# TensorE runs on the identity until the operands come, four key tiles are begun with their first halves, and three steps of the first batch trade places

## Chip, cores and metric

One core of one Trainium2 chip. The metric is the time of one execution on the device, in microseconds. TensorE (PE in the profile) multiplies, ScalarE (ACT) and VectorE (DVE) do the element work, GpSimd (POOL) fills and scatters, SyncE (SP) issues most of the loads.

## What is computed

A gated cross-attention layer and a layer of experts, all in fp32:

```python
def layer(x, ctx):                     # x: 16 x 100 x 512, ctx: 16 x 722 x 512
    q = (layernorm(x) @ Wq.T + bq)     # 16 heads of 32
    k, v = ctx @ Wk.T + bk, ctx @ Wv.T + bv
    o = softmax(q @ k.T / sqrt(32) + mask) @ v
    x = x + tanh(g_xattn) * (o @ Wo.T + bo)
    h = layernorm(x)
    gates = softmax(h @ gate_w + gate_b)         # 8 experts, the best 2 of each row
    y = w3[e] @ gelu(w2[e] @ gelu(w1[e] @ h + b1[e]) + b2[e]) + b3[e]
    return x + tanh(g_ffn) * sum(gates[e] * y for e in best_two)
```

## The kernel before

A stage for attention runs over 16 batches of 100 queries and 722 context rows, and a stage for the experts follows. Each engine has its own program, written out in order by hand; semaphores join them. Nothing is planned at run time in the stretch at hand.

**Products.** An fp32 product is made of three faster ones: each operand is split into a high part (a ScalarE copy, `w_high`, `ctx_high`, `k_high`) and a low part (a VectorE subtraction of the high part, `wk_low`, `ctx_low`, `k_low`), and `PRODUCTS` names the three pairs. So a key tile, 128 rows of K.T by one half of the context (362 or 360 columns), is 4 pieces `c` of the 512 inputs by 3 products: 12 matmuls into one bank of PSUM. `FRONT` are the first two pieces and `BACK` the last two. A value tile is 12 matmuls of 512 columns. Transposes and the query products are plain fp32; in the trace a plain fp32 matmul has two records and two weight loads.

**Units and banks.** Of the 8 banks, four (0 to 3) take the scores of the four heads of a group, two (4, 5) the transposed probabilities, and two (6, 7) everything else: the units. A unit is one such result: `K20` is key tile 2 of context half 0, `V1` value tile 1, `XT` the transposed normed rows, `Q` the queries, `A2` the attention output of group 2. `PROLOGUE`, `FIRST_BODY`, `EVEN_BODY` and `ODD_BODY` list them in order, and the loop below them gives each its bank, alternately, and its number of fill. TensorE waits in `bank_for` until the unit before in that bank has been emptied; for a key tile that is after ScalarE's `keys_high` and VectorE's `keys_low`. In the prologue `XT` and `Q` have a third bank, score bank 0, which is free until the first scores.

**Prologue.** It makes the keys, three value tiles and the queries of batch 0. SyncE asks for the first half of the key weights, the first two pieces of the context, the second half of the weights, the other two pieces, then the value weights, the second half of the context, the rows `x_ln` to be normed, and so on. ScalarE and VectorE split them in that order: `w_lo` counts the low halves of the weights (1 and 2 for the keys, 3 and 4 for the values), `ctx_lo` those of the context. TensorE waits for `w_lo` 1 and `ctx_lo` 1, runs `FRONT` of key tiles 0 and 1, waits for `w_lo` 2 and `ctx_lo` 2, runs their `BACK`, then tiles 2 and 3 whole. GpSimd makes the 128x128 identity `ident` in its first instructions (`ident_step` 2).

**A batch.** Four groups of four heads. For each: `scores` for each context half into four banks, VectorE's `score` takes them out, adds the mask and finds the maximum; ScalarE's `exps`, one for each head; TensorE's `transpose_probs`, which needs the `copy_probs` of the head before, as there is one pair of banks for it; and `attend`. Between them TensorE has the next batch's key and value tiles as filling. `scores` of a half wait until VectorE has taken out the half before. In batch 0 the order around the change is:

- ScalarE, heads 8 to 11: `keys_high` of tile 2, `copy_probs` 10 and 11, `rstd_start(0, 2)` (logarithm and exponential of the variance of batch 2's rows), `keys_high` of tile 0, half 1.
- VectorE: `wo_lower` (low part of the output weights, a whole 128x2048), `keys_low` of tile 2, `norm_in(2)` (statistics of batch 2's rows), `recips(2)`, `keys_low` of tile 0 half 1, `ln_apply(0, 2)` (three steps on one column, and the normed rows `xn`), then the scores of group 3.
- ScalarE, heads 12 to 15: `copy_probs` 13, `keys_high` of tile 1 half 1, `exps` 15, `copy_probs` 14 and 15.

SyncE loads batch 2's rows `x_ln` once batch 1's are normed. GpSimd, once for each of the first score groups, starts a transfer of 3341 KB that fills a region of the expert rows.

Of the kernel before, what the change touches and what calls it, by code (L numbers as in the profile page):

```python
# [16 lines left out]
P = 128  # L17
# [195 lines left out]
             "A0", "A1", "X2T", "A2", "LG", "CNT")  # L213
LAST_TURNS = LAST_BODY.index("A0")
PRO = -1
SAME_BANK = {("LG", "A1"), ("CNT", "A2"), ("XT", "A2")}


ALL_UNITS = {}
FILLS = [0, 0, 0]  # L220
_next = 0
for body in range(PRO, B + 1):
    _names = {PRO: PROLOGUE, 0: FIRST_BODY, B - 2: LAST_QUERIES, B - 1: LAST_BODY, B: AFTER_LAST
              }.get(body, ODD_BODY if body % 2 else EVEN_BODY)
    for _i, name in enumerate(_names):
        if _i > 0 and (_names[_i - 1], name) in SAME_BANK:
            _next = 1 - _next
        if body >= B - 1:
            _bank = _i % 2 if body == B else (_i + 1) % 2 if _i < LAST_TURNS else 0
        elif body == PRO and name in ("XT", "Q"):  # L230
            _bank = 2
        else:
            _bank, _next = _next, 1 - _next
        FILLS[_bank] += 1
        ALL_UNITS[body, name] = _bank, FILLS[_bank]
# [36 lines left out]
def attention(nc, sem, shared_from, bank_rows, banks, ident, block_expert, block_row, early,  # L272
              xs_dram, x, ctx_in, mask, g_x, g_f, wq, bq, wk, bk, wv, bv, wo, bo, gw, gb, out,
              w1, b1, w2, b2, w3, b3):
    score_bank, pt_bank, unit_bank = banks[0:4], banks[4:6], banks[6:8] + banks[0:1]

    bk_loaded = sem("bk_loaded")
    bv_loaded = sem("bv_loaded")
# [21 lines left out]
    xres_loaded = sem("xres_loaded")  # L300
    ctx_hi = sem("ctx_hi")
    ctx_lo = sem("ctx_lo")
    filled = [sem("unit_bank_0_filled"), sem("unit_bank_1_filled"), sem("first_queries_filled")]
    emptied = [sem("unit_bank_0_emptied"), sem("unit_bank_1_emptied"), sem("first_queries_emptied")]
    k_hi = sem("k_hi")
    ln_step = [sem("ln1_step"), sem("ln2_step")]
    ln_log = [sem("ln1_log"), sem("ln2_log")]
# [347 lines left out]
    def on_tensor(pe):  # L655
# [314 lines left out]
        def last_body(b, odd):  # L970
# [76 lines left out]
            for m in range(4, HT):  # L1047
                early_second(m)

        pe.wait_ge(ident_step, 2)  # L1050
        pe.wait_ge(pt_zero, 1)
        pe.wait_ge(w_lo, 1)
        pe.wait_ge(ctx_lo, 1)
        keys(PRO, 0, 0, 0, FRONT)
        keys(PRO, 0, 1, 0, FRONT)
        pe.wait_ge(w_lo, 2)
        pe.wait_ge(ctx_lo, 2)
        keys(PRO, 0, 0, 0, BACK)
        keys(PRO, 0, 1, 0, BACK)
        keys(PRO, 0, 2, 0)  # L1060
        keys(PRO, 0, 3, 0)
        pe.wait_ge(w_lo, 4)
        values(PRO, 0)
        values(PRO, 1)
# [14 lines left out]
    def on_scalar(act):  # L1079
# [29 lines left out]
        def keys_high(body, n, m, half):  # L1109

            if n > 0:
                act.wait_ge(scores_ready, 2 * DT * (n - 1) + 2 * m + half + 1)
            bank, _ = take(body, f"K{m}{half}")
            off, size = HALVES[half]
            nc.scalar.activation(k_hl[0][:, m, off:off + size], bank[:, 0:size], ACT.Identity,  # L1115
                                 bias=bk_sb[:, m:m + 1]).then_inc(k_hi, 1)
# [45 lines left out]
        def first_body():  # L1162

            b, n = 0, 1
            half_used(PRO, "V2")
            ctx_high(n, 0)
            ctx_high(n, 1)
            keys_high(b, b, 3, 1)
            exps(b, 0)
            exps(b, 1)  # L1170
            copy_probs(b, 0)
            exps(b, 2)
            copy_probs(b, 1)
            exps(b, 3)
            copy_probs(b, 2)
            copy_probs(b, 3)
            rstd_start(0, 1)

            half_used(b, "V5")
            ctx_high(n, 2)  # L1180
            ctx_high(n, 3)
            recip_copy(b, 0)
            exps(b, 4)
            exps(b, 5)
            copy_probs(b, 4)
            exps(b, 6)
            copy_probs(b, 5)
            exps(b, 7)
            keys_high(b, n, 0, 0)
            copy_probs(b, 6)  # L1190
            copy_transposed(b, "XS", xt[:, :, slot(1), :])
            copy_probs(b, 7)
            wo_upper()

            keys_high(b, n, 1, 0)
            recip_copy(b, 1)
            exps(b, 8)
            exps(b, 9)
            copy_probs(b, 8)
            exps(b, 10)  # L1200
            copy_probs(b, 9)
            exps(b, 11)
            keys_high(b, n, 2, 0)
            copy_probs(b, 10)
            copy_probs(b, 11)
            rstd_start(0, 2)
            keys_high(b, n, 0, 1)

            keys_high(b, n, 3, 0)
            copy_transposed(b, "XT", xt[:, :, slot(2), :])  # L1210
            recip_copy(b, 2)
            exps(b, 12)
            exps(b, 13)
            queries_high(b, "Q01")
            copy_probs(b, 12)
            exps(b, 14)
            copy_probs(b, 13)
            keys_high(b, n, 1, 1)
            exps(b, 15)
            copy_probs(b, 14)  # L1220
            copy_probs(b, 15)
            keys_high(b, n, 2, 1)

# [182 lines left out]
    def on_vector(dve):  # L1406
# [288 lines left out]
        def first_body():  # L1695
# [27 lines left out]
            score(b, 2, 1)  # L1723
            scale_o(b, b, 1)
            values_out(b, 1, 2)
            wo_lower()
            keys_low(b, n, 2, 0)
            norm_in(2)
            recips(b, 2)
            keys_low(b, n, 0, 1)  # L1730
            ln_apply(0, 2, x_ln[:], xn[:], xn_ready)

            score(b, 3, 0)
            keys_low(b, n, 3, 0)
            score(b, 3, 1)
            scale_o(b, b, 2)
            queries_low(b, "Q01")
            keys_low(b, n, 1, 1)
            recips(b, 3)
            keys_low(b, n, 2, 1)  # L1740
# [983 lines left out]
```

## Time and profile before

| | us |
|---|---|
| median of 3 runs (lowest, highest) | 1788.13 (1786.92, 1789.49) |
| profiled execution | 1788.08 |
| its span | 1786.1 |
| TensorE busy in the span | 1760.7 |
| VectorE busy | 1168.8 |
| ScalarE busy | 961.6 |

Times in the profile are counted from the start of the span. The profiled execution took 2.0 us more than its span. Busy time of TensorE includes matmuls that overlap, so it doesn't tell how near the engine is to its peak; the spacing of the starts does.

### The profile page before, as it was taken

Reading aid. Unit: us, or ns where it says so; the run is one execution under the profiler, and the core shown is the slowest. Engines: PE = TensorE matmul, PEld = TensorE weight load, DVE = VectorE, ACT = ScalarE, POOL = GpSimd, SP = SyncE. Lnnn points to the kernel's source line nnn. Section 1 sums busy time; section 2 is a strip of 40 time slices with the busy share of each in tenths; the row PEclk is TensorE's granted clock in tenths of the full one; section 3 lists DMA queues with packets and bytes.
Section 4 is the critical chain, followed back from the end, with each engine's and each line's share of the span. In section 5 each row is a group of like instructions: output and inputs, shape, how many; then the busy total and the mean of one; then the engine's idle time right before and its main releaser. Section 6 shows DMA issues by size and latency. Waiting matters only on the chain.

```text
span 1786.1 us, 39483 instructions
## 1 busy us (share of the span) xinstructions
PE 1760.7 (99%) x14832; PEld 1530.9 (86%) x14832; DVE 1168.8 (65%) x3158; ACT 961.6 (54%) x1794; POOL 119.6 (7%) x159
## 2 busy tenths in 40 slices
PE   8999999999999999999999999999999999999997
PEld 7788888888888888888888877877899999999996
DVE  5666666666667666666666456556677777777772
ACT  4565655555565656555555535445555555455551
POOL 1000000000000000000000010100001111111110
PEclk9999999999999999999999999999999999999999
DMA  7991111111111211111103489999666666767761
GB/s 244 338 336 43 48 49 42 48 48 52 38 48 49 59 38 48 48 49 47 40 16 95 152 278 396 372 346 310 212 209 206 212 209 217 217 217 217 213 199 36
DMA packets 114267, 269.72 MB, mean 151 GB/s; under 512 B 15283, under 2 KB 33715, under 8 KB 114128
## 3 DMA queue, kind: packets, MB, share of 16 engines
q1 hardware_dynamic: 99664, 225.46, 38.0%
q0 software_dynamic: 14464, 42.35, 8.2%
q8 instruction: 94, 1.54, 0.4%
q14 instruction: 45, 0.37, 0.1%
HBM read 221.10 MB, written 46.66 MB: 150 GB/s over the span
## 4 chain that ended last, share of the span: by engine, by line
PE 95%; DMA 2%; DVE 1%; ACT 1%; issue 1%; POOL 0%; DVEq 0%; SPq 0%; ACTq 0%; POOLq 0%
PE bank_rows L2304 21%; PE bank_rows L688 15%; PE bank_rows L674 15%; PE bank_rows L736 8%; PE bank_rows L2319 6%; PE bank_rows L726 5%; PE bank_rows L747 4%; PE bank_rows L2358 4%; PE bank_rows L2385 3%; PE bank_rows L2344 3%; PE bank_rows L711 3%; PE bank_rows L763 3%; PE bank_rows L826 2%; DMA stage<-in_L_ffn_w 1%; PE bank_rows L750 1%; PE bank_rows L812 1%
## 5 line engine op out<-in xcount | busy, mean ns | idle before, releaser
L1139 ACT ACTIVATE probs<-probs,neg_max 100x722 f32<-100x722 f32 x248 | 220.9, 891 | 101.0 <-DVE neg_max L1491 101.0
L1484 DVE CUSTOM_DVE_ANT_0 probs<-bank_rows,mask_sb 100x362 f32<-100x362 f32 x496 | 234.6, 529 | 11.5 <-PE bank_rows L726 7.2
L2548 DVE TENSOR_TENSOR w_low<-stage,w_high 128x1024 fp32r<-128x1024 f32 x176 | 212.9, 1223 | 33.9 <-ACT w_high L2452 32.9
L1144 ACT ACTIVATE p_t<-bank_rows 121x600 f32<-121x600 f32 x256 | 171.9, 672 | 77.4 <-PE bank_rows L736 73.9
L2475 ACT ACTIVATE gelu<-bank_rows,biases 128x256 f32<-128x256 f32 x176 | 82.4, 475 | 222.9 <-PE bank_rows L2304 189.5
L2452 ACT ACTIVATE w_high<-stage 128x1024 fp32r<-128x1024 f32 x176 | 183.7, 1057 | 31.4 <-DMA stage<-in_L_ffn_w 31.4
L2304 PE MATMUL bank_rows<-h_low,w_high 128*128 128x256 f32 x704 | 199.2, 283 | 0.0
L2304 PE MATMUL bank_rows<-h_high,w_low 128*128 128x256 f32 x704 | 199.2, 283 | 0.0
L2304 PE MATMUL bank_rows<-h_high,w_high 128*128 128x256 f32 x704 | 199.2, 283 | 0.0
L674 PE MATMUL bank_rows<-ctx_high,wk_high 128*128 128x360 f32 (+1 forms) x512 | 183.8, 359 | 8.6 <-DVE ctx_low L1450 8.1
L736 PE MATMUL bank_rows<-ident,probs 100*121 100x100 f32 x1488 | 180.6, 257 | 1.6 <-ACT p_t L1144 1.4
L736 PEld LDWEIGHTS bank_rows<-ident,probs 100*121 100x121 f32 x1488 | 160.4, 156 | 23.6 <-issue 2.2
L674 PE MATMUL bank_rows<-ctx_low,wk_high 128*128 128x360 f32 (+1 forms) x512 | 168.9, 330 | 0.0
L674 PE MATMUL bank_rows<-ctx_high,wk_low 128*128 128x360 f32 (+1 forms) x512 | 168.4, 329 | 0.0
L1457 DVE SCALAR_TENSOR_TENSOR k_low<-bank_rows,bk_sb,k_high 128x362 fp32r<-128x362 f32 (+1 forms) x128 | 76.1, 594 | 131.3 <-ACT k_high L1115 117.1
L688 PE MATMUL bank_rows<-wv_high,ctx_high 128*120 128x512 f32 (+1 forms) x384 | 161.7, 421 | 0.0
L688 PE MATMUL bank_rows<-wv_high,ctx_low 128*120 128x512 f32 (+1 forms) x384 | 151.1, 394 | 0.0
L688 PE MATMUL bank_rows<-wv_low,ctx_high 128*120 128x512 f32 (+1 forms) x384 | 151.0, 393 | 0.0
L2304 PEld LDWEIGHTS bank_rows<-h_high,w_low 128*128 128x128 f32 x704 | 135.2, 192 | 0.0
L2304 PEld LDWEIGHTS bank_rows<-h_high,w_high 128*128 128x128 f32 x704 | 135.1, 192 | 0.0
L2304 PEld LDWEIGHTS bank_rows<-h_low,w_high 128*128 128x128 f32 x704 | 135.1, 192 | 0.0
L1115 ACT ACTIVATE k_high<-bank_rows,bk_sb 128x362 fp32r<-128x362 f32 (+1 forms) x128 | 72.0, 563 | 112.7 <-PE bank_rows L674 112.7
(244 smaller groups left out, 3718.8 us busy)
## 6 DMA issues: line engine op xcount, KB each, us to landing
stage<-in_L_ffn_w SPq DMA_DIRECT2D x240, 512.0 KB, 4.5
plain_w<-in_L_ffn_w SPq DMA_DIRECT2D x15, 2048.0 KB, 12.3
expert_in_rows<-filling POOLq DMA_DIRECT2D x8, 3341.0 KB, 15.2
ctx_raw<-in_ctx SPq DMA_DIRECT2D x16, 720.0 KB, 4.9
ctx_raw<-in_ctx SPq DMA_DIRECT2D x15, 724.0 KB, 4.3
xs_sb<-expert_in_rows SPq DMA_DIRECT2D x11, 514.0 KB, 5.1
b_sb<-in_L_ffn_b SPq DMA_DIRECT2D x19, 256.0 KB
mask_sb<-in_mask_BxSxS_ff SPq DMA_DIRECT2D x16, 282.0 KB
```

Source lines behind the costliest of these rows:

```text
L674: last = nc.tensor.matmul(bank[:, 0:size], wk_hl[a][:, c, m * P:(m + 1) * P], ctx_t[b][half][:, c, :], start=(c == 0 and s == 0), stop=(c ...
L688: last = nc.tensor.matmul(bank[0:rows, :], ctx_t[a][half][:, c, off:off + rows], wv_hl[b][:, c, :], start=(c == 0 and s == 0), stop=(c == ...
L726: last = nc.tensor.matmul(score_bank[q][0:S, 0:size], q_t[a][rows, g, slot(b), :], k_hl[c][rows, g, off:off + size], start=(step == 0), st ...
L736: last = nc.tensor.transpose(pt_bank[i // 3][0:rows, i % 3 * S:(i % 3 + 1) * S], probs_of(b, h // HQ)[:, h % HQ, off:off + rows], ident[0: ...
L1139: nc.scalar.activation(p, p, ACT.Exp, bias=neg_max[:, h:h + 1], scale=-1.0, accum_out=exp_sum[:, h:h + 1]).then_inc(probs_ready, 1)
L1144: nc.scalar.activation(p_t[:, h % HQ, :, :].rearrange("t (k i) s -> t k (i s)", k=2), bank_rows[0:TT, 4:6, 0:3 * S], ACT.Copy).then_inc(pt ...
L1484: nc.vector.tensor_tensor_reduce(out=probs_of(b, g)[:, q, at], in0=score_bank[q][0:S, 0:size], in1=mask_sb[:, at], scale=-1.0, scalar=BIG, ...
L2304: last = nc.tensor.matmul(mm_bank[m % 4][:, 0:BLOCK], w[a][:, k, m * P:(m + 1) * P], src[c][:, k, :], start=(k == 0 and s == 0), stop=(k = ...
L2319: last = nc.tensor.matmul(y_bank[t][:], h_hl[1][a][:, k, t * P:(t + 1) * P], w_hl[2][c][:, k, :], start=(k == 0 and s == 0), stop=(k == HT ...
L2452: nc.scalar.activation(hi, src, ACT.Copy).then_inc(chunk_hi[which], 1)
L2475: nc.scalar.activation(gelu[:, m % 2, :], mm_bank[m % 4][:, 0:BLOCK], ACT.Gelu, bias=bias_of(n, layer, m)).then_inc(g_done, 1)
L2548: nc.vector.tensor_tensor(lo, src, hi.bitcast(F32), ALU.subtract).then_inc(chunk_lo[which], 1)
```

## The change

- A run-up: once the identity is made, TensorE multiplies it by itself 15 times into score bank 3. Nothing reads the result.
- `K20` and `K30` of the prologue get banks of their own, score banks 0 and 1, so that four key tiles are open at once. All four are begun with `FRONT`, then all four are finished with `BACK`. `XT` and `Q` follow in score bank 0.
- Batch 0, VectorE: `norm_in(2)` goes ahead of tile 2's `keys_low`, `ln_apply(0, 2)` ahead of `recips(2)` and of tile 0's `keys_low`, and `wo_lower` behind `queries_low`.
- Batch 0, ScalarE: `rstd_start(0, 2)` goes ahead of `copy_probs` 10, and tile 1's `keys_high` behind `copy_probs` 14.

```diff
--- before.py
+++ after.py
@@ -213,11 +213,12 @@
              "A0", "A1", "X2T", "A2", "LG", "CNT")
 LAST_TURNS = LAST_BODY.index("A0")
 PRO = -1
+RUN_UP = 15
 SAME_BANK = {("LG", "A1"), ("CNT", "A2"), ("XT", "A2")}
 
 
 ALL_UNITS = {}
-FILLS = [0, 0, 0]
+FILLS = [0, 0, 0, 0]
 _next = 0
 for body in range(PRO, B + 1):
     _names = {PRO: PROLOGUE, 0: FIRST_BODY, B - 2: LAST_QUERIES, B - 1: LAST_BODY, B: AFTER_LAST
@@ -227,8 +228,8 @@
             _next = 1 - _next
         if body >= B - 1:
             _bank = _i % 2 if body == B else (_i + 1) % 2 if _i < LAST_TURNS else 0
-        elif body == PRO and name in ("XT", "Q"):
-            _bank = 2
+        elif body == PRO and name in ("K20", "K30", "XT", "Q"):
+            _bank = 3 if name == "K30" else 2
         else:
             _bank, _next = _next, 1 - _next
         FILLS[_bank] += 1
@@ -272,7 +273,7 @@
 def attention(nc, sem, shared_from, bank_rows, banks, ident, block_expert, block_row, early,
               xs_dram, x, ctx_in, mask, g_x, g_f, wq, bq, wk, bk, wv, bv, wo, bo, gw, gb, out,
               w1, b1, w2, b2, w3, b3):
-    score_bank, pt_bank, unit_bank = banks[0:4], banks[4:6], banks[6:8] + banks[0:1]
+    score_bank, pt_bank, unit_bank = banks[0:4], banks[4:6], banks[6:8] + banks[0:2]
 
     bk_loaded = sem("bk_loaded")
     bv_loaded = sem("bv_loaded")
@@ -300,8 +301,9 @@
     xres_loaded = sem("xres_loaded")
     ctx_hi = sem("ctx_hi")
     ctx_lo = sem("ctx_lo")
-    filled = [sem("unit_bank_0_filled"), sem("unit_bank_1_filled"), sem("first_queries_filled")]
-    emptied = [sem("unit_bank_0_emptied"), sem("unit_bank_1_emptied"), sem("first_queries_emptied")]
+    filled = [sem("unit_bank_0_filled"), sem("unit_bank_1_filled"), sem("unit_bank_2_filled"), sem("unit_bank_3_filled")]
+    emptied = [sem("unit_bank_0_emptied"), sem("unit_bank_1_emptied"),
+               sem("unit_bank_2_emptied"), sem("unit_bank_3_emptied")]
     k_hi = sem("k_hi")
     ln_step = [sem("ln1_step"), sem("ln2_step")]
     ln_log = [sem("ln1_log"), sem("ln2_log")]
@@ -1047,18 +1049,19 @@
             for m in range(4, HT):
                 early_second(m)
 
+
         pe.wait_ge(ident_step, 2)
+        for _ in range(RUN_UP):
+            nc.tensor.matmul(score_bank[3][:, 0:P], ident[:], ident[:], start=True, stop=True)
         pe.wait_ge(pt_zero, 1)
         pe.wait_ge(w_lo, 1)
         pe.wait_ge(ctx_lo, 1)
-        keys(PRO, 0, 0, 0, FRONT)
-        keys(PRO, 0, 1, 0, FRONT)
+        for m in range(DT):
+            keys(PRO, 0, m, 0, FRONT)
         pe.wait_ge(w_lo, 2)
         pe.wait_ge(ctx_lo, 2)
-        keys(PRO, 0, 0, 0, BACK)
-        keys(PRO, 0, 1, 0, BACK)
-        keys(PRO, 0, 2, 0)
-        keys(PRO, 0, 3, 0)
+        for m in range(DT):
+            keys(PRO, 0, m, 0, BACK)
         pe.wait_ge(w_lo, 4)
         values(PRO, 0)
         values(PRO, 1)
@@ -1201,9 +1204,9 @@
             copy_probs(b, 9)
             exps(b, 11)
             keys_high(b, n, 2, 0)
+            rstd_start(0, 2)
             copy_probs(b, 10)
             copy_probs(b, 11)
-            rstd_start(0, 2)
             keys_high(b, n, 0, 1)
 
             keys_high(b, n, 3, 0)
@@ -1215,9 +1218,9 @@
             copy_probs(b, 12)
             exps(b, 14)
             copy_probs(b, 13)
-            keys_high(b, n, 1, 1)
             exps(b, 15)
             copy_probs(b, 14)
+            keys_high(b, n, 1, 1)
             copy_probs(b, 15)
             keys_high(b, n, 2, 1)
 
@@ -1723,18 +1726,18 @@
             score(b, 2, 1)
             scale_o(b, b, 1)
             values_out(b, 1, 2)
-            wo_lower()
+            norm_in(2)
             keys_low(b, n, 2, 0)
-            norm_in(2)
+            ln_apply(0, 2, x_ln[:], xn[:], xn_ready)
             recips(b, 2)
             keys_low(b, n, 0, 1)
-            ln_apply(0, 2, x_ln[:], xn[:], xn_ready)
 
             score(b, 3, 0)
             keys_low(b, n, 3, 0)
             score(b, 3, 1)
             scale_o(b, b, 2)
             queries_low(b, "Q01")
+            wo_lower()
             keys_low(b, n, 1, 1)
             recips(b, 3)
             keys_low(b, n, 2, 1)
```

## Rows read from the trace of the kernel before

**Rows 1.** The page: the chain of waits by engine, and the instruction queue.

```profile
q8 instruction: 94, 1.54, 0.4%
...
PE 95%; DMA 2%; DVE 1%; ACT 1%; issue 1%; POOL 0%; DVEq 0%; SPq 0%; ACTq 0%; POOLq 0%
```

**Rows 2.** What TensorE waited for in all: us in total, times, longest us.

```profile
PE bank_rows L726 <- DVE half_max L1484: 1.4, 2, 1.2
...
PE bank_rows L747 <- issue: 1.1, 1, 1.1
```

**Rows 3.** Timeline of TensorE, 7.9 to 15.5 us: start, us, what, idle before.

```profile
8.13 0.64 PE L674 MATMUL bank_rows<-ctx_high,wk_high 128*128 128x362 f32 x1 [8.13 <-DVE ctx_low L1450]
...
12.79 0.43 PE L674 MATMUL bank_rows<-ctx_high,wk_high 128*128 128x362 f32 x1
...
14.92 0.43 PE L674 MATMUL bank_rows<-ctx_high,wk_high 128*128 128x362 f32 x1 [0.36 <-DVE k_low L1457]
```

**Rows 4.** Windows in the prologue: us, busy (count) of PE, PEld, DVE, ACT, POOL, clock, DMA.

```profile
8.20:12.70 4.50, 4.50 (x15) 4.50 (x16) 3.61 (x4) 3.21 (x4) 0.00 (x0) 1.00 1.04 349
14.92:19.01 4.09, 4.09 (x24) 4.09 (x25) 2.92 (x4) 2.19 (x4) 0.00 (x0) 1.00 1.06 350
```

**Rows 5.** Timeline of all engines, 0 to 30 us.

```profile
1.28 0.29 POOL L481 TENSOR_SCALAR_AFFINE_SELECT ident<-ident 128x128 f32<-128x128 f32 x1 [0.24 <-POOL ident L479]
...
7.04 0.94 DVE L1450 TENSOR_TENSOR ctx_low<-ctx_raw,ctx_high 128x724 fp32r<-128x724 f32 x1
...
9.71 0.91 DVE L1450 TENSOR_TENSOR ctx_low<-ctx_raw,ctx_high 128x724 fp32r<-128x724 f32 x1
...
11.14 2.43 DVE L1867 TENSOR_TENSOR wv_low<-wq_sb,wv_high 128x1024 fp32r<-128x1024 f32 x2 [0.52 <-ACT wv_high L1373]
```

**Rows 6.** Chain of waits, 1129 to 1137 us: start, us, what.

```profile
1133.03 3.57 PE bank_rows L2344 x32
```

**Rows 7.** DMA of 0 to 60 us in 40 slices; one load, last number us to landing.

```profile
DMA  0599999979999999889865000004999999999999
...
wq_sb<-in_L_xattn_Wq SPq DMA_DIRECT2D x1, 1024.0 KB, 8.6
```

**Rows 8.** Chain of waits, 36 to 110 us.

```profile
80.63 0.78 PE bank_rows L736 x6
...
83.18 0.06 DVE k_low L1457
...
83.69 0.22 DVE rstd L1429
...
84.78 0.53 DVE probs L1484
...
86.83 0.74 PE bank_rows L726 x11
```

**Rows 9.** Timeline of ScalarE and VectorE, 76 to 88 us.

```profile
76.37 2.28 DVE L1693 TENSOR_TENSOR wo_low<-wo_sb,wo_high 128x2048 fp32r<-128x2048 f32 x1
...
79.81 0.67 ACT L1144 ACTIVATE p_t<-bank_rows 121x600 f32<-121x600 f32 x1
...
82.00 0.29 ACT L1103 ACTIVATE rstd<-moments,eps 100x1 f32<-100x1 f32 x1
...
82.32 0.20 ACT L1106 ACTIVATE rstd<-rstd 100x1 f32<-100x1 f32 x1
```

**Rows 10.** Timeline of ScalarE and TensorE, 94 to 98 us.

```profile
96.41 0.66 ACT L1144 ACTIVATE p_t<-bank_rows 121x600 f32<-121x600 f32 x1
...
97.22 0.77 PE L736 MATMUL bank_rows<-ident,probs 100*121 100x100 f32 x6 [0.64 <-ACT p_t L1144]
```

**Rows 11.** Timeline of SyncE's issues, 56 to 62 us.

```profile
57.47 0.32 SPq L597 DMA_DIRECT2D x_ln<-in_x  x1
```

**Rows 12.** DMA of 26 to 130 us: packets and MB of the queue; median us to landing.

```profile
q8 instruction: 7, 0.11, 0.4%
...
ctx_raw<-in_ctx SPq DMA_DIRECT2D x2, 724.0 KB, 13.1
```

## Prediction

> **What bounds the kernel now.** I read the page first. Its chain of waits says that TensorE sets the end: 95% of the chain is TensorE work [rows 1]. Then the waits of TensorE: after the first matmul has begun, its engine loses time to others in only a few places [rows 2], all of them before 98 us. The queries for 100 to 962 us name none. From there to the end the kernel is a sequence that is started by TensorE's own progress (loads wait on counters of finished work), so what TensorE gains before 98 us should reach the end unchanged. The question is then only how much earlier its instruction stream runs at 98 us.
>
> The timeline of TensorE shows two losses in the prologue. The first matmul starts at 8.13 us, when the first low half of the context is ready, and the 15 next ones stand 0.300 us apart; after 12.79 us, that is 4.66 us of work, they stand closer, and from 14.92 us there are 24 in 4.09 us, 0.170 each [rows 3, 4]. 362 columns in 0.300 us is the 1.2 GHz level, the faster spacing the 2.4 GHz level. The granted clock column says 1.00 in both stretches [rows 4], so here the spacing must be read, not the column. Second, at 14.92 us the key tiles 2 and 3 wait for the banks of tiles 0 and 1 (0.36 us idle in the row) [rows 3].
>
> **The prologue.** The run-up needs only the identity, done at 1.57 us [rows 5]. No row shows an identity matmul of this form, but the first layer of the small expert blocks has the same shape, fp32 128x128 by 128x128: 32 records in 3.57 us, two records per matmul, so 0.223 us each at the fast level [rows 6] and 0.446 us at half of that. If the clock rises 4.66 us after the start as it did before, the run-up takes 4.66 us for 10.4 matmuls and 4.6 x 0.223 = 1.03 us for the rest. It begins near 1.65 us and ends near 7.3 us, under the wait for the context's low half, which ends at 7.04 + 0.94 = 7.98 us [rows 5]. It adds nothing to the path. The bound on the other side: all 15 slow is 6.7 us, to 8.34 us, 0.2 us late. It writes a score bank that nothing uses before the first scores, moves no DMA and makes no other engine wait.
>
> Does anything feed the faster keys? First halves of four tiles are 24 matmuls, 4.09 us, to 12.22 us. The second halves need the second low half of the context, ready at 9.71 + 0.91 = 10.62 us [rows 5]: 1.6 us to spare. That is what the reordering buys: with only two tiles begun, fast matmuls would be through at about 10.2 us and stand. The four tiles hold four banks, so the wait at 14.92 us has no bank to wait for. The last 24 end at 8.13 + 8.18 = 16.31 us, against 19.01 us before [rows 4]. The gain is 2.70 us.
>
> What is late next? The values need both low halves of their weights, done at 11.14 + 2.43 = 13.57 us [rows 5], and the bank of tile 0, whose sum is complete at 13.24 us and which two copies of 0.6 us empty by about 14.6 us. Both lie ahead of 16.31 us. ScalarE and VectorE then do the copies of tiles 2 and 3 behind the second half of the context, until about 18.3 us, then the statistics; nothing takes those tiles' banks before the first transposed rows at about 26 us. TensorE has no idle time between 19 and 38 us before. The one thing that could stand still is the transfers, as they don't come earlier by this change. The DMA share by slices of 1.5 us is 0 from the 23rd slice (33 us) on, so every load asked for before has landed by about 33.5 us [rows 7]. VectorE's check for the last small loads now comes near 35.3 us (before: 38 us) and is still behind that. The query weights (1 MB) are used from 28.4 instead of 31.04 us; they are asked for when the values' weights are split, near 13.6 us, and take 8.6 us to land, so they are there near 22 us [rows 7]. I count 2.70 us, all kept. Ends for this term: 0.7 (clock slow again, below) and 2.9 (48 at the spacing inside a burst, 0.166).
>
> **Batch 0, statistics moved up.** The chain of waits shows why TensorE stands 1.2 us before the scores of group 3: VectorE gets to those scores late, at 84.78 us. It does the low key half at 83.18, and only then the layer norm's four small steps from 83.69 on, about 1.1 us [rows 8]. The low split of the output weights (2.28 us from 76.37 us) and a key copy had kept it from the statistics until 80.5 us [rows 9]. In the changed order the statistics run at 76.4 us, in the place of the split, and the norm is applied at about 80.6 us, while VectorE would wait for ScalarE anyway. The split goes behind the query halves, into idle time near 93.4 to 95.7 us, and its result is needed only in the next batch.
>
> This isn't free on ScalarE. The two statistics functions (0.29 and 0.20 us, 0.51 with the step between them) run there and now stand ahead of the copy of head 10, which began at 79.81 us; head 11's transposes began at 80.63 us, 0.15 us behind that copy's end [rows 8, 9]. So they slip to 81.14 us, and the key half behind them too: its VectorE copy goes from 83.18 to 83.69, and the group's scores on VectorE start at 84.20 instead of 84.78 us. TensorE's next scores follow at 86.25 instead of 86.83 us. TensorE's own work before them ended at 86.83 - 1.2 = 85.6 us [rows 2, 8] and ends 0.51 later now, at 86.1 us, so both arrive together. A wait of 1.2 us is replaced by one of 0.5 us earlier and 0.1 us here: gain 0.58 us. Ends: 0 (a copy I overlook) and 1.1 (if the copy of head 10 isn't held up).
>
> **Batch 0, one key copy moved down.** Before, ScalarE ran a key copy (near 95.1 us) ahead of the exponentials of head 15. The copy of head 14 then ended at 97.07 us, and head 15's transposes stood 0.64 us [rows 10]. In the new order the exponentials start near 94.6 us, the copy of head 14 ends near 96.3 us, and TensorE reaches the transposes at 96.58 us without a wait: gain 0.64 us, at most that. The key copy moves to about 96.2 us; its bank is taken again by the first key tile of the next batch some 2 us later. The split in front of its VectorE half ends before it.
>
> **Sum.** 2.70 + 0.58 + 0.64 = 3.92 us from the profiled execution's 1788.08 us (span 1786.1 and 2.0 around it) is 1784.2 us. The median of the runs is 1788.13 us, 0.05 above, which changes nothing. About 0.2%, 3.6 us, is what a measurement can tell from no change; the forecast lies just beyond it.
>
> **A rule that speaks against it.** The first 4.66 us of dense work were slow in the one execution that I have [rows 3], which doesn't say how far that moves between runs. The Trainium skill (TensorE: Matmul & The Clock Gate, "What's actually happening") says that the point at which the clock rises varies, because the chip's activity check runs free of the kernel's start, and that idle time throttles again. By the rule the run-up might end late, which costs 0.2 us, or the gap after it might undo it, which is the second rival.
>
> **Rivals.** (1) As forecast, 1784.2 us, own range 1783.4 to 1785.0.
> (2) The clock is at 1.2 GHz again, or still, when the keys begin, after the 0.8 us gap behind the run-up. Then 15.5 keys take 4.66 us and 32.5 take 5.53, to 18.3 us: gain 0.7 instead of 2.70, 1786.2 us. Against it: after the 1.2 us wait of [rows 2] the scores' 11 matmuls take 0.74 us [rows 8], with no slow stretch.
> (3) Batch 0 gives nothing back: the added ScalarE work ahead of head 10 costs what the rest brings, or the norm's rows aren't there. 1785.4 us. The load was issued at 57.47 us [rows 11] and is now needed 19 us behind its issue instead of 23; the bigger context loads of that stretch took 13.1 us in the median [rows 12]. It would have to take over 19 us to be felt at all.
> (4) TensorE stood 1.1 us near 72 us with no releaser, in the middle of a run of small matmuls, the row of [rows 2] with 1.1 us. The page counts 94 instruction transfers of 1.54 MB, 16 KB each [rows 1]. If the wait is a late one of these, the run-up's 60 or so instructions (two weight loads and two matmuls for each of 15) shift every block against the program. It may vanish: 1784.2 - 1.1 = 1783.1 us.
> (5) The other side: the same mechanism at more places. Seven transfers of that queue fall between 26 and 130 us, where DMA is busiest [rows 12]. At 1.1 us for each that comes late, four more (4.4 us) eat the whole gain; six more give 1784.2 + 6.6 = 1790.8 us, slower. For it: the shift is certain. Against: before, one of the seven stood. The Trainium skill (Runtime: NRT & Kernel Launch, "Instruction fetch mechanics") says blocks of 16 KiB are fetched ahead and mostly hidden; the page's sizes agree.
>
> **Chances.** (1) 0.60, (2) 0.08, (3) 0.12, (4) 0.12, (5) 0.08, half of it to beyond the old time. Faster by over 0.2% means under 1784.6 us: four fifths of (1), all of (4), 0.60 together. Slower by over 0.2%: 0.04. The rest, 0.36, lies within. The range takes in (2) and (3) above and (4) below, each with the half microsecond that runs differ: 1782.4 to 1787.0 us; (5) stays outside.
>
> **What would show it.** Right: 30 identity records between 1.6 and 7.5 us, with a step in their spacing near 6.3 us; the first key at 8.13 us, its successors 0.166 apart; the values at 16.3 us instead of 19.01; the first scores near 34.7 instead of 37.4 us; in batch 0 the wait before the scores of group 3 nearly gone and a new one of half a microsecond before head 11's transposes; the wait before head 15's gone. Wrong: keys 0.300 apart after 8.13, a first key later than 8.4 us, TensorE rows with idle time and no releaser, or a gain at 98 us that isn't found at 962 us.

## The result, and the profile after

| | before | changed |
|---|---|---|
| median of 7 runs (lowest, highest), us | 1787.97 (1786.92, 1789.49) | 1781.53 (1781.32, 1782.14) |
| profiled execution, span | 1788.08, 1786.1 | 1782.03, 1780.0 |
| ratio to before | | 0.9965, 95% interval 0.9955 to 0.9975 |

The change makes the kernel 6.4 us faster by the medians and 6.1 us by the two profiled executions. I had forecast 3.9 us, and 1782.4 us as the low end. The direction came out, and so did the two mechanisms that I had counted; the size did not. Part of the 6.4 us is how the seven runs of the kernel before fell: in the three larger sets (17, 28 and 33 runs) that ran beside the kernels below its median is 1787.2 to 1787.5 us, which leaves 5.7 to 6.0 us.

First what TensorE waits for in the changed kernel, in the form of [rows 2]:

```profile
PE bank_rows L1055 <- POOL ident L483: 1.6, 1, 1.6
PE bank_rows L738 <- ACT p_t L1147: 1.3, 2, 0.8
PE bank_rows L676 <- DVE ctx_low L1453: 0.7, 1, 0.7
...
PE bank_rows L728 <- DVE half_max L1487: 0.2, 1, 0.2
```

The wait of 1.2 us for the scores of group 3 is gone from this list; the 0.2 us that are left in its row are another one, at 37.57 us, and were there before too (the two waits of 1.4 us in [rows 2] are 1.2 and 0.2). The stand, as I call the 1.1 us in which TensorE stood without a releaser, is gone. The timeline of TensorE at the start, with the line numbers of the changed kernel (two or three above those before):

```profile
1.62 5.72 PE L1055 MATMUL bank_rows<-ident 128*128 128x128 f32 x30 [1.62 <-POOL ident L483]
8.04 0.40 PE L676 MATMUL bank_rows<-ctx_high,wk_high 128*128 128x362 f32 x1 [0.70 <-DVE ctx_low L1453]
8.28 0.33 PE L676 MATMUL bank_rows<-ctx_low,wk_high 128*128 128x362 f32 x1
...
12.12 0.32 PE L676 MATMUL bank_rows<-ctx_high,wk_high 128*128 128x362 f32 x1
...
16.12 0.39 PE L690 MATMUL bank_rows<-wv_high,ctx_high 128*121 128x512 f32 x1
```

The run-up ends at 1.62 + 5.72 = 7.34 us, the first key stands within 0.1 us of where it stood in [rows 3], and from the second on the keys are 0.167 us apart (the second halves follow at 12.12 us without a break). The values begin at 16.12 us instead of 19.01. The windows over the run-up and the keys, in the form of [rows 4]:

```profile
1.62:6.00 4.38, 4.38 (x20) 4.38 (x21) 0.19 (x1) 1.75 (x3) 3.18 (x18) 1.00 0.80 277
6.20:7.30 1.10, 1.10 (x11) 0.95 (x9) 1.10 (x2) 0.27 (x1) 0.97 (x1) 1.00 1.02 324
8.04:16.12 8.08, 8.08 (x48) 8.08 (x49) 6.18 (x7) 5.97 (x8) 0.00 (x0) 1.00 1.00 321
```

20 records in 4.38 us are 0.219 us each and 11 in 1.10 us are 0.100 each (the starts of the records themselves are 0.213 and 0.112 us apart): the 1.2 GHz level and then the 2.4 GHz level. The clock column says 1.00 for both, as in [rows 4]. The chain of waits in batch 0, to be held against [rows 8]:

```profile
67.21 1.17 PE bank_rows L749 x48
...
75.59 0.19 ACT rstd L1106
...
75.81 0.20 ACT rstd L1109
76.01 0.57 ACT p_t L1147
...
76.71 0.77 PE bank_rows L738 x6
...
81.73 0.08 issue
81.81 0.74 PE bank_rows L728 x10
```

and head 15's transposes in the timeline, without a wait:

```profile
91.27 0.32 PE L676 MATMUL bank_rows<-ctx_high,wk_low 128*128 128x360 f32 x1
...
91.44 0.77 PE L738 MATMUL bank_rows<-ident,probs 100*121 100x100 f32 x6
```

The attention output of group 1 is one run of 48 records in 1.17 us. The statistics functions are now in the chain ahead of the copy of head 10, and head 11's transposes start at 76.71 us behind a wait of 0.52. Then TensorE works up to the scores of group 3 and loses 0.08 us there instead of 1.2.

Laid beside each other, the two traces differ by 2.9 us at the first value (19.01, 16.12), 4.3 us behind the attention output of group 1 (72.94, 68.62), 5.0 us at the scores of group 3 (86.83, 81.81), 5.8 us at the transposes of head 15 (97.22 in [rows 10], 91.44), 5.8 us at the queries of batch 14 (947.02, 941.26) and 6.1 us at the end.

### The profile page after: what moved, and what is told of

It reads as the page before. It is cut to its first block, busy times and chain, and to the rows that moved or that the text cites. A ratio compares the mean times of both kernels' runs of the same rounds, so it can differ in the third digit from the quotient of the medians.

```text
span 1780.0 us, 39543 instructions
## 1 busy us (share of the span) xinstructions
PE 1763.5 (99%) x14862; PEld 1534.2 (86%) x14862; DVE 1168.4 (66%) x3158; ACT 961.1 (54%) x1794; POOL 113.9 (6%) x159
## 4 chain that ended last, share of the span: by engine, by line
PE 96%; DMA 2%; DVE 1%; ACT 1%; issue 0%; POOL 0%; DVEq 0%; SPq 0%; ACTq 0%; POOLq 0%
PE bank_rows L2307 21%; PE bank_rows L690 16%; PE bank_rows L676 15%; PE bank_rows L738 8%; PE bank_rows L2322 7%; PE bank_rows L728 5%; PE bank_rows L749 4%; PE bank_rows L2361 4%; PE bank_rows L2388 3%; PE bank_rows L2347 3%; PE bank_rows L713 3%; PE bank_rows L765 3%; PE bank_rows L828 2%; DMA stage<-in_L_ffn_w 1%; PE bank_rows L752 1%; PE bank_rows L814 1%
```

## The experiments

Theory A, at the start: the 1.4 us between the first value and the attention output of group 1 are a block of TensorE's instructions that came late before, and the run-up's instructions moved the borders of the blocks. Rival B: they come from the moved steps. Rivals C (whether the stand comes is chance in the queues) and D (the clock's rise varies from execution to execution too) came up on the way.

**One part of the change each.** `prologue_only` has the run-up and the four tiles and batch 0 in its old order, `batch0_only` the opposite.

> The changed kernel with batch 0 in its old order. The changed kernel's trace shows 2.9 us of the gain at the first value tile, 1.4 us more at the attention output of group 1 of batch 0, where TensorE had stood without a releaser, and 1.3 us in the moved steps. Theory A: the 1.4 us is a 16 KB block of TensorE's instructions that came late before, and the run-up's instructions shift the block borders; then this run gains 2.9 + 1.4 = 4.3 us on the kernel before (about 1783.7 us) and the stand without a releaser is gone. Theory B: the stand went away because of the moved steps in batch 0; then this run gains 2.9 us only and still has it.

> The kernel before with the moved steps of batch 0 alone. Both theories give the moved steps 1.2 to 1.3 us. Theory A: the stand of 1.1 to 1.4 us without a releaser near 72 us stays, 1.2 us gained in all (about 1786.7 us). Theory B: it is gone, 2.6 us gained.

```diff
+        for _ in range(15):          # runup_only: this loop alone
+            nc.tensor.matmul(score_bank[3][:, 0:P], ident[:], ident[:], start=True, stop=True)
-        keys(PRO, 0, 0, 0, FRONT)   # tiles_only: these lines and the two banks alone
-        keys(PRO, 0, 1, 0, FRONT)
+        for m in range(DT):
+            keys(PRO, 0, m, 0, FRONT)
...                                  # and the four BACK halves in the same way
```

> The kernel before with the run-up alone. The keys run at the fast level from 8.1 us, but the first halves of two tiles are through near 10.1 us, the second halves wait for the context's second low half (10.6 us), and tile 2 waits for the copies of tile 0, which stand behind the values' split on VectorE until 13.6 us: tile 2 begins near 14.3 us, the values near 18.4 instead of 19.0 us, 0.6 us gained. Theory A adds 1.4 us, since the block borders move by the run-up's instructions: 2.0 us. If the run-up alone gave the 2.9 us, the four open tiles would be needless.

> The kernel before with the four open key tiles alone, no run-up. The clock rises near 12.8 us as before, and nothing waits for a bank: values near 18.2 us, 0.8 us gained. Theory A: the block borders hardly move (the same matmuls, one wait more or less), so the stand near 72 us stays, 0.8 us in all. If the stand goes here too, the time at which TensorE gets there matters more than where the borders lie.

| kernel | median us, runs | ratio to before, interval | values start | stand | first value to queries of batch 14 |
|---|---|---|---|---|---|
| prologue_only | 1783.46, 11 | 0.9978 (0.9969, 0.9987) | 16.09 | none | 926.56 |
| batch0_only | 1786.28, 11 | 0.9990 (0.9981, 0.9999) | 19.16 | 1.07 | 926.55 |
| runup_only | 1785.58, 11 | 0.9989 (0.9980, 0.9998) | 17.96 | none | 926.56 |
| tiles_only | 1786.43, 11 | 0.9994 (0.9985, 1.0003) | 18.31 | none | 926.58 |

B falls: with the moved steps alone the stand is there. The waits of TensorE in `batch0_only`:

```profile
PE bank_rows L747 <- issue: 1.1, 1, 1.1
```

The last column is the point. From the first value to the queries of batch 14 TensorE's stream is the same in all kernels, so only stands and waits can differ. With the old order and no stand it is 926.6 us; with the stand 928.0 (the first trace of before: 947.02 - 19.01); `batch0_only` has the stand and the moved steps and comes to 926.55, so stand and moved steps cancel; the changed kernel has 925.14. So the stand costs 1.4 us and the moved steps give 1.4 to 1.5. The run-up and the four tiles need each other. With the run-up alone the keys are fast from the start, but TensorE waits 1.2 us for a bank before tile 2 (the row of 0.9 us is the one before the first key, at 8.07 us, which the changed kernel has too, with 0.7),

```profile
PE bank_rows L674 <- DVE k_low L1459: 1.2, 1, 1.2
PE bank_rows L674 <- DVE ctx_low L1452: 0.9, 1, 0.9
```

and with the tiles alone the slow stretch stays. But `tiles_only` hardly moves a border and has no stand, which A did not foresee; that speaks for C.

**Borders and traffic.** Three kernels for the stand, one for the price of the moved statistics.

```diff
         pe.wait_ge(ident_step, 2)
+        for _ in range(60):          # before_pad60; 196 in the changed kernel for after_pad196
+            pe.wait_ge(ident_step, 2)
-            pool.wait_ge(scored, 6 * e + 1)
+            pool.wait_ge(scored, 6 * e + (7 if e > 1 else 1))      # fills_later
-            rstd_start(0, 2)
             copy_probs(b, 10)
+            rstd_start(0, 2)         # copy10_first, on the changed kernel
```

> The kernel before with 60 waits that are already met at the head of TensorE's program, ended long before the operands come at 8 us. They move the borders of its instruction blocks by about as much as the run-up does and change nothing else in time. Theory A (where the borders lie against the program decides): no stand without a releaser near 72 us, 1.1 to 1.4 us gained. Theory C (it is chance in the queues: the block's transfer stands behind the fill of a region that has just begun, and whether it does varies): the stand may be there or not, and the median lies anywhere from 0 to 1.4 us below the kernel before, with the same spread of the single runs of about 3 us. The four runs so far speak for C: with the four tiles alone the borders hardly moved, and the block's transfer was served at 60 us instead of 70, with no stand.

> The changed kernel with 196 such waits at the head of TensorE's program, so that with the run-up's 60 instructions the borders are moved by one whole block of 256 and lie as in the kernel before. Theory A: the stand comes back in the middle of the attention output of group 1, 1.1 to 1.4 us slower than the changed kernel (about 1783 us). Theory C: 1781.5 us in most runs, now and then more. If the waits take so long that the run-up starts late, it shows in the run-up's own rows.

> The kernel before with the fills of the regions from the third on started one score group later, so that none begins near 58 us. Both theories have the block's transfer behind the fill's traffic as the cause of its lateness: the block of the middle of batch 0 is served within a few us of its request, no stand near 72 us, 1.1 to 1.4 us gained unless a later fill delays a later block. If the stand stays, the fills are not what the block waits behind.

> The changed kernel with the copy of head 10 ahead of the two statistics functions on ScalarE, where they fill the wait for head 11's transposes. My sum of the moved steps says that their place costs TensorE 0.5 us (it stood 0.52 us there in the changed kernel's trace) and that nothing needs them before VectorE's norm, which would now start 0.5 us later but still ahead of the low key half. So 0.4 to 0.6 us faster than the changed kernel, about 1781.0 us. Rival: the wait before the scores of group 3 comes back as far as the other one shrinks, 1781.5 us.

`before_pad60`: 1787.11 us, ratio 0.9997 (0.9988 to 1.0006), no stand in its trace. `fills_later`: 1786.97 us, 0.9999 (0.9990 to 1.0008), no stand. The medians cannot tell either from the kernel before, so its own traces had to be looked at again (below). `after_pad196` missed its aim: 1791.46 us, 1.0023 (1.0014 to 1.0032). Its timeline says why:

```profile
12.19 5.29 PE L1057 MATMUL bank_rows<-ident 128*128 128x128 f32 x30 [12.19 <-issue]
17.23 0.41 PE L676 MATMUL bank_rows<-ctx_high,wk_high 128*128 128x362 f32 x1
```

The waits began when the identity was ready, at 1.6 us, and took until 12.19 us, 54 ns for each one written, so the run-up began 10.6 us late and all that follows with it. The aim was missed in a second way, too. The trace counts 902 semaphore instructions of TensorE against 804 in the changed kernel, 98 more and not 196, and 834 for `before_pad60` against 804 before, 30 more and not 60: two waits that are written one behind the other stand there as one. So against the kernel before the borders moved by 98 and the run-up's 60, 158 instructions, not by the 256 that the expectation wanted, and did not come back to where they lay before. Where few loads run, before 400 us, three blocks in a row are served after 2076, 2193 and 2336 matmuls of the kernel before, and in `after_pad196`, the run-up's not counted, after 2030, 2137 and 2273. That there was no stand says nothing about A, then.

`copy10_first`: 1781.46 us, 0.9968 (0.9955 to 0.9980). The wait of 0.52 us before head 11's transposes is gone, the stretch from first value to batch 14 is 924.79 instead of 925.14 us, 0.35 shorter; that is less than the 0.4 to 0.6 that I had expected, and the median does not show it.

**More traces of the kernel before, a shorter run-up, one more moved copy.**

```diff
-RUN_UP = 15
+RUN_UP = 8                           # runup8
-            keys_high(b, n, 0, 0)
             copy_probs(b, 6)
+            keys_high(b, n, 0, 0)    # copy6_too, on copy10_first
```

> The kernel with the copy of head 10 first, and also with the copy of head 6 ahead of the key copy of tile 0 in group 1, the same kind of step as the one that the change makes in group 3. TensorE stood 0.78 us before head 7's transposes for that copy in every trace so far. 0.5 to 0.8 us faster than the kernel with the copy of head 10 first, about 1780.8 us. Rival: ScalarE's key copy is then late for VectorE's low half, and the next score wait takes it back.

> The changed kernel with 8 identity matmuls instead of 15. They end near 5.2 us, all at the slow level, and TensorE then stands 2.9 us. In the before-like traces the clock rose 3.0 to 5.1 us behind the first matmul. If the rise has to come while TensorE works, some executions begin the keys at the slow level: spread of the single runs like that of the kernel before (about 3 us) and the median 0.5 to 2 us above the changed kernel. If 3.6 us of work are enough and 2.9 us of rest don't undo them, it equals the changed kernel, 1781.5 us with a spread of 0.8.

> The kernel before once more, for a second trace of it. Theory D: both the point at which the clock rises and the stand near 72 us differ from execution to execution; the first value tile starts anywhere from 18.0 to 19.2 us, and the stand of 1.1 us may be missing. Theory A: the trace repeats the first one, values at 19.0 us and the stand there.

> A third trace of the kernel before, with the same expectation as the second: by theory D another point of the rise and perhaps no stand, by theory A the same again.

> A fourth trace of the kernel before. The three so far: values at 19.0 and 18.7 us with the stand near 72 us (1788.1 and 1788.2 us), values at 18.1 us without it (1786.1 us). If the stand hangs on how late TensorE is, then values after about 18.5 us come with a stand and over 1787.5 us, and values before that come without and under 1786.7 us. If both are independent chance, the pairs will mix.

> A fifth trace of the kernel before: the same rule as for the fourth.

> A sixth trace of the kernel before: the same rule. If one of the three lies above 1789 us, its trace should show a still later rise of the clock or a second stand.

> A second trace of the changed kernel: run-up over before 8.1 us wherever the clock rises, values at 16.1 us, no stand, 1781.3 to 1782.1 us. A stand or values later than 16.3 us would say that the change only moved the chances.

| trace | time us | values start | stand | block served at, after how many matmuls | queries of batch 14 | span |
|---|---|---|---|---|---|---|
| before, first | 1788.08 | 19.01 | 1.06 | 69.9, 425 | 947.02 | 1786.1 |
| before_a | 1788.24 | 18.71 | 1.06 | 69.8, 429 | 946.76 | 1786.3 |
| before_b | 1786.14 | 18.07 | none | 60.4, 357 | 944.65 | 1784.2 |
| before_c | 1787.36 | 18.72 | 1.07 | 69.8, 429 | 946.70 | 1785.5 |
| before_d | 1788.37 | 18.67 | 1.34 | 69.9, 433 | 946.92 | 1786.3 |
| before_e | 1787.70 | 19.24 | none | 65.2, 383 | 945.83 | 1785.8 |
| changed, first | 1782.03 | 16.12 | none | 57.6, 379 | 941.26 | 1780.0 |
| after_b | 1781.26 | 16.04 | none | 57.7, 380 | 941.15 | 1779.3 |

The block is the transfer of the instruction queue that lands between 57 and 70 us; the count is that of TensorE's matmul records up to then. Both the values' start and the block vary in the kernel before, as theory D had it, and the stand is there in four traces of six. They do not go together: `before_e` has the latest values and no stand. My rule for the three last traces, late values with a stand, held in two (and `before_c` took 1787.36 us, not over 1787.5).

What separates the traces is the block of that queue just before, served at 51.0 and 53.9 us in the two without a stand and at 55.0 to 55.3 in the four with it; why it varies is open. The start of the values is not the clock alone either: in `before_b` and `before_c` the clock rises at the same 10.9 us, but tile 2 waits 0.36 us for its bank in the one and 1.06 in the other, where VectorE's low halves of the second weights and context came 0.9 us later.

The point of the rise, in the timelines of `before_b` (first) and `before_e` (second):

```profile
10.62 0.50 PE L674 MATMUL bank_rows<-ctx_high,wk_low 128*128 128x362 f32 x1
10.92 0.38 PE L674 MATMUL bank_rows<-ctx_high,wk_high 128*128 128x362 f32 x1
11.13 0.33 PE L674 MATMUL bank_rows<-ctx_low,wk_high 128*128 128x362 f32 x1
```

```profile
13.29 0.50 PE L674 MATMUL bank_rows<-ctx_high,wk_low 128*128 128x362 f32 x1
13.59 0.45 PE L674 MATMUL bank_rows<-ctx_high,wk_high 128*128 128x362 f32 x1
13.87 0.34 PE L674 MATMUL bank_rows<-ctx_low,wk_high 128*128 128x362 f32 x1
```

The starts close up from 0.30 to 0.17 us behind 10.9 us in the one and behind 13.6 in the other, 2.9 and 5.6 us after the first key. The stand itself, in the chain of `before_d`, where the run of 48 small matmuls of [rows 2] is torn, and in `before_b`, where it is whole:

```profile
69.76 1.15 PE bank_rows L747 x42
...
72.26 0.37 PE bank_rows L747 x6
```

```profile
69.17 1.17 PE bank_rows L747 x48
```

That the stand is this block come late is worked out, not seen: in all five traces with a stand (`batch0_only` is the fifth) the block had not been served when TensorE had issued 425 matmuls, TensorE stopped behind the 467th and no other, and went on 2.2 to 2.4 us after the block's service had begun; with the same borders and the block served by the 393rd matmul, TensorE did not stop. DMA was full whether the block came early or late. The windows of the DMA view around the service, of `before_a` (69.7 to 69.9 us) and of the changed kernel (57.5 to 57.7): queue, packets, MB, share of 16 engines in 0.2 us:

```profile
q0 software_dynamic: 14, 0.06, 76.3%
q1 hardware_dynamic: 15, 0.02, 31.5%
q8 instruction: 1, 0.02, 28.8%
```

```profile
q0 software_dynamic: 16, 0.07, 102.6%
q8 instruction: 1, 0.02, 35.4%
```

`fills_later` had its previous block at 54.6 us, nearly as late as the traces with a stand (55.0 to 55.5), and the next was served at 65.9 instead of 69.8, with the fill of 3341 KB that starts at 58 us taken away. That does not show that the block waits behind the fill: `before_e`, with the fill in place, had its blocks at 53.9 and 65.2 us, the same 11.3 us apart. That it waits behind traffic of some kind is likely: in `fills_later` the last packet of the loads ended at 65.5 us, and the block followed at 65.9 with nothing else under way.

`runup8`: 1784.69 us, 0.9986 (0.9977 to 0.9995), the single runs from 1783.25 to 1785.91. Neither of the two outcomes that I had described, but a third. Its timeline:

```profile
1.62 3.78 PE L1055 MATMUL bank_rows<-ident 128*128 128x128 f32 x16 [1.62 <-POOL ident L483]
7.98 0.40 PE L676 MATMUL bank_rows<-ctx_high,wk_high 128*128 128x362 f32 x1 [2.58 <-DVE ctx_low L1453]
8.23 0.33 PE L676 MATMUL bank_rows<-ctx_low,wk_high 128*128 128x362 f32 x1
...
8.89 0.33 PE L676 MATMUL bank_rows<-ctx_high,wk_low 128*128 128x362 f32 x1
9.06 0.43 PE L676 MATMUL bank_rows<-ctx_high,wk_high 128*128 128x362 f32 x1
9.29 0.51 PE L676 MATMUL bank_rows<-ctx_low,wk_high 128*128 128x362 f32 x1
9.59 0.51 PE L676 MATMUL bank_rows<-ctx_high,wk_low 128*128 128x362 f32 x1
...
12.31 0.44 PE L676 MATMUL bank_rows<-ctx_high,wk_low 128*128 128x362 f32 x1
12.59 0.33 PE L676 MATMUL bank_rows<-ctx_high,wk_high 128*128 128x362 f32 x1
12.75 0.33 PE L676 MATMUL bank_rows<-ctx_low,wk_high 128*128 128x362 f32 x1
```

The keys begin at the fast level, 0.167 us apart, and after the seventh, at 9.06 us, they fall to 0.30 until 12.3 us. TensorE had rested 2.58 us in front of them. The changed kernel rests 0.70 us there and keeps its clock. So it is not enough that there is a run-up. Whether its length counts (16 records, 0.213 us apart but for the first, so none at the fast level) or the rest behind it, this run cannot say, as it changes both. The values start at 17.59 us, 1.5 us later than in the changed kernel; the median is 3.2 us higher, partly because the stretch from batch 14 to the end is longer too (839.6 against 838.5 us, below).

`copy6_too`: 1781.65 us, 0.9970 (0.9959 to 0.9981), 924.49 us from first value to batch 14, again 0.3 us less than `copy10_first` where I had expected 0.5 to 0.8, and again not in the median.

**The borders once more.** The kernel with 60 idle waits, twice again:

> A second trace of the kernel before with 60 met waits at the head of TensorE's program. The kernel before had the stand near 72 us in four of six traces. If moving the block borders by 60 instructions protects from it, it is missing here as in the first trace; if it is chance alone, it appears in two of three such traces.

> A third trace of the same kernel with the same expectation. No stand in three of three traces would have a chance of 1 in 27 if it came in two of three.

1786.07 and 1786.09 us, values at 18.48 and 18.62 us, the block served at 60.3 and 60.6 us, no stand in either. With the first that makes three of three, and the eight traces that have a run-up have none either, against four of six before. If the stand came in two of three executions, three without it would have a chance of 1 in 27. So A is supported, not proven, as far as it says that moving the borders, here by 30 instructions, protects from the late block. C stands as far as it says that before it was chance. With `tiles_only` there is a single trace, so whether it escaped by chance is open.

## Why the forecast fell short

**The clock at the start: right.** The run-up ended at 7.34 us (forecast 7.3), the first key was not late, the four tiles never stood, the values began at 16.12 us (forecast 16.31). The first trace of before began them at 19.01; the mean of six is 18.74. The gain is 2.6 to 2.9 us, forecast 2.70. `prologue_only` has it with batch 0 in its old order, and neither the run-up alone (values at 17.96 us) nor the tiles alone (18.31) nor a run-up of 8 (17.59) does. My tail case, a run-up that is slow throughout, is nearly what `copy10_first` shows (6.34 us, ended at 7.96), and it costs nothing.

The rule of the Trainium skill (TensorE: Matmul & The Clock Gate, "What's actually happening") held in kind: the point of the rise varies between runs, and in `runup8` the clock fell again behind a rest. In size it did not: that section gives the variation as 500 ns to either side, and in the six traces of the kernel before the point lies between 10.9 and 13.6 us, 2.7 us apart. As a threat it was the wrong way round: the slow stretch and its variation were a cost of the kernel before, which the run-up hides. It does not follow that the single runs draw together for that reason: those of the changed kernel spread over 0.8 us against 2.6, but those of `prologue_only`, with the same run-up and tiles, over 2.4.

**The moved steps: mis-sized by 0.2 us.** Forecast 0.58 + 0.64 = 1.22 us, measured 1.45 (926.57 to 925.12 us). The places are as forecast: the wait for the scores of group 3 gone but for 0.08 us, one of 0.52 us before head 11's transposes (forecast 0.5). The first term is 0.70 in place of 0.58: the transposes slipped by 0.40 us (from 4.32 us ahead of before to 3.92), not by 0.51, as the two functions put the copy of head 10 off by 0.44 us only (from 0.44 to 0.88 us behind the start of the key copy ahead of it). The second is 0.79 in place of 0.64, which I had called the most that it could give: a row counts a wait from the modelled end of the matmul before it, and without a wait the next one starts 0.15 us ahead of that end (91.44 us, where the key matmul ahead of it ends at 91.27 + 0.32 = 91.59). So the same wait costs 0.15 us more than its row says. Of the 0.70 + 0.79 us, 0.04 are lost again before the queries of batch 14.

**The stand: the step that failed.** The prediction counted the stand near 72 us as kept and gave its vanishing 12%, at 1.1 us. The mechanism of rivals 4 and 5 was right in kind, and there was even a reason in my own text (the run-up's instructions shift every block), but I took the sign as open. It went in all eight traces with a run-up, and it had cost 1.4 us, more than its row of 1.06: the run of 48 small matmuls took 2.6 us (70.12 to 72.71) instead of 1.17. As it is there in four traces of six, with 1.4 to 1.7 us in the stretch from the first value to batch 14, it is worth 1.0 us in the mean (927.58 to 926.58). With rival 4 the outcome would still have been put 1.6 us too high, at 1783.1 us.

**From batch 14 to the end: the second step that failed.** "What TensorE gains before 98 us should reach the end unchanged" held to the queries of batch 14. The rest was taken to be started by TensorE's own progress, although the page gave 2% of the chain, some 36 us, to DMA [rows 1]. From there to the end of the span the six traces of before take 838.8 to 840.0 us, 839.4 in the mean; the six that have both the run-up of 15 and the four tiles take 838.1 to 838.8, 838.5 in the mean. That is 0.9 us that no step of mine holds. All of it lies in the first expert work, between about 1000 and 1270 us; from there to the last matmul all twenty traces take the same 504.67 us, to 0.01. The chain of the first trace of before, 1040 to 1110 us, runs there through two loads of expert weights,

```profile
1056.55 7.38 PE bank_rows L2344 x64
...
1075.29 12.63 DMA stage<-in_L_ffn_w
...
1090.48 10.56 DMA stage<-in_L_ffn_w
...
1106.55 3.50 PE bank_rows L2344 x29
```

and that of `after_b` over the same stretch through TensorE alone:

```profile
1050.68 7.35 PE bank_rows L2347 x64
...
1069.82 3.57 PE bank_rows L2347 x32
...
1100.09 3.57 PE bank_rows L2347 x32
```

From the 64 matmuls to the last group shown it is 50.0 us in the one and 49.4 in the other. Why the loads come in time there is open. The first trace of the changed kernel still has them in its chain, at 49.9 us, so this does not go with the change alone.

Together: 2.65 (mean of the values' start, 18.74 to 16.08) + 1.0 + 1.45 + 0.9 = 6.0 us, against 6.05 us between the mean spans (1785.7 and 1779.65). The parts are cut from the same traces, so that they close is no proof of their causes.

What the account cannot do: `before_pad60` has no stand in three traces, yet its median over 11 runs lies only 0.1 us below that of the kernel before beside it, with an interval of 1.6 us either way, and that of `fills_later` 0.3 us. By the means it is 0.5 us for both, about half of the 1.0. Whether the timed runs had the stand, and how often, is not known, so the 1.0 us rests on traces alone.

A slip in the sum of the range: half a microsecond beyond (4) and (2) is 1782.6 and 1786.7 us, not 1782.4 and 1787.0. The result lies outside either.

## What to carry over

Where TensorE sits idle before its first operands, dense dummy work that ends just ahead of them brings the clock up at no cost that these runs show. Check that nothing then makes the fast engine wait (here the four open tiles), and that the rest between the two stays short (0.70 us did no harm, 2.58 us behind a shorter run-up did). Before costing a change against one trace, take several of the kernel before: here the start of the values and a stand of 1.4 us differed between executions. A wait with no releaser inside a run of small matmuls can be a late instruction block, which a change in the number of instructions ahead of it may remove. And read how many instructions an edit adds from the trace, not from the source: 196 waits were 98.

## What the hardware showed that I had not expected

- A 16 KB block of instructions was served at 69.9 us in the first trace of before, 8 us behind the point in the program at which `before_b` had it (the 357th matmul, passed near 61.4 us), while a fill of 3341 KB and the context loads kept the DMA engines full. In the traces with so late a block TensorE stood for 1.06 to 1.34 us.
- The clock fell from its 2.4 GHz to its 1.2 GHz level in the middle of dense work, 1.1 us after the work had begun again behind a rest of 2.58 us.
- 196 waits that are already met cost TensorE 10.6 us, 54 ns each; in the trace they are 98 semaphore instructions, mostly 0.106 us apart.
